# MetaFormer block: groups that stay on their partitions, scores and values in halves

## The reference

```python
x = x + conv(_ln_c(x))             # layer norm over the last axis, j
t = x.reshape(16, 1024, 32)
t = t + ffn(_ln_t(t))              # layer norm over the last axis again

def conv(x, Wq, Wk, Wv, rq, rk, rv, Gq, Gk, Gv1, Gv2):
    q, k, v = (einsum('oc,ncij->noij', W_, x) for W_ in (Wq, Wk, Wv))
    qk  = einsum('ncij,nchj->nihj', q, k) / d
    qrq = einsum('ncij,chi->nihj', q, rq) / d
    krk = einsum('ncij,chi->nihj', k, rk) / d
    weight = softmax(qk + Gq * qrq + Gk * krk, axis=3)      # over j
    return (einsum('nihj,nchj->ncij', weight, Gv1 * v)
            + einsum('nihj,chi->ncij', weight, Gv2 * rv))

def ffn(x, W, V, gamma, beta):
    wx = batch_norm(x @ W.T) * gamma + beta    # statistics over all 16 * 1024 tokens
    yt = sigmoid(wx[:, t] + yt @ V.T)          # one step for each of the 1024 tokens, in order
```

## Time and profile before

| what | value |
|---|---|
| median of three runs | 146.82 us (145.81 to 147.19) |
| the profiled execution's own time | 145.42 us |
| its span in the trace | 143.6 us |
| PE busy | 100.2 us (70%) |
| DVE busy | 99.0 us (69%) |
| ACT busy | 66.0 us (46%) |
| POOL busy | 61.1 us (43%) |

### The profile page before, as it was taken

The page is one execution under the profiler, slowest core; times in us unless marked ns, Lnnn a source line. Parts: engine busy times, 40 slices in busy tenths (PEclk is TensorE's granted clock), DMA queues, the critical chain, the costliest instruction groups (busy, mean ns, idle before and its releaser), DMA issues.

```text
span 143.6 us, 4286 instructions
## 1 busy us (share of the span) xinstructions
PE 100.2 (70%) x1830; PEld 68.2 (47%) x1830; DVE 99.0 (69%) x153; ACT 66.0 (46%) x142; POOL 61.1 (43%) x72
## 2 busy tenths in 40 slices
PE   0697995999299001999975656933998888999200
PEld 0332231388299001999964545301232337999200
DVE  5898838067103899937750199899659879788992
ACT  7958775900063025284030015233533379999300
POOL 8985928840000188990000069982430000005940
PEclk9999999999999955599999999996589999999955
DMA  4892987588800000334642000000000000000667
GB/s 147 264 261 20 208 204 161 132 216 187 205 6 5 5 2 2 77 92 112 164 106 54 5 5 5 0 0 5 0 0 0 0 0 0 5 0 0 188 190 208
DMA packets 9823, 11.63 MB, mean 81 GB/s; under 512 B 2828, under 2 KB 6924, under 8 KB 9804
## 3 DMA queue, kind: packets, MB, share of 16 engines
q1 hardware_dynamic: 9228, 10.31, 28.0%
q10 hardware_dynamic: 576, 1.05, 3.2%
HBM read 2.97 MB, written 2.10 MB: 35 GB/s over the span
## 4 chain that ended last, share of the span: by engine, by line
DVE 29%; PE 27%; ACT 12%; issue 10%; POOL 8%; SPq 6%; DMA 5%; POOLq 0%; ACTq 0%; DVEq 0%
PE ps L1022 6%; PE ps L1001 6%; PE ps L1033 5%; ACT warm L653 5%; PE ps L1055 4%; DVE xin L355 4%; DVE att_tile L742 3%; PE ps L1044 3%; POOL y_tile L433 3%; DVE bn L824 3%; DVE y_tile L361 3%; POOL y_tile L187 3%; SPq L290 3%; DMA xin<-in_x_dram 3%; DMA spread<-att_tile 2%
## 5 line engine op out<-in xcount | busy, mean ns | idle before, releaser
L361 POOL TENSOR_TENSOR y_tile<-xin,u_tile 128x256 f32<-128x256 f32 (+1 forms) x7 | 7.1, 1052 | 24.2 <-DVE xin L355 24.2
L1022 PE MATMUL ps<-w_bd,y_tile 128*32 128x128 f32 x256 | 9.1, 313 | 10.0 <-DVE att_tile L742 10.0
L411 POOL TENSOR_TENSOR att_tile<-att_tile,soft 128x1024 f32<-128x1024 f32 x4 | 7.7, 1914 | 19.5 <-DVE soft L748 19.5
L1055 PE MATMUL ps<-rel_tile,w_bd 128*128 128x512 f32 x16 | 11.1, 806 | 5.2 <-DVE rel_tile L820 5.1
L1022 PEld LDWEIGHTS ps<-w_bd,y_tile 128*32 128x32 f32 x256 | 8.5, 169 | 10.5 <-DVE att_tile L742 10.2
L590 ACT ACTIVATE square<-y_tile 128x512 f32<-128x512 f32 x8 | 5.0, 628 | 18.0 <-POOL y_tile L433 15.9
L1044 PE MATMUL ps<-spread,v_tile 128*32 128x64 f32 x512 | 8.9, 223 | 6.1 <-issue 6.1
L893 DVE TENSOR_SCALAR ps<-att_tile,bnv 128x512 f32<-128x512 f32 x15 | 11.0, 807 | 1.6 <-ACT warm L653 1.6
L1044 PEld LDWEIGHTS ps<-spread,v_tile 128*32 128x32 f32 x512 | 8.1, 109 | 6.9 <-issue 6.9
L1095 PE MATMUL ps<-blank 128*128 128x512 bf16 x48 | 11.3, 382 | 0.0
L968 PE MATMUL ps<-xin 128*128 128x512 f32 x18 | 10.8, 749 | 0.0
(11 more groups left out here) (107 smaller groups left out, 236.7 us busy)
## 6 DMA issues: line engine op xcount, KB each, us to landing
out_dram<-y_tile SPq DMA_DIRECT2D x8, 256.0 KB, 2.4
xin<-in_x_dram SPq DMA_DIRECT2D x3, 512.0 KB, 5.0
spread<-att_tile SPq DMA_DIRECT2D x12, 128.0 KB, 2.5
v_tile<-u_tile SPq DMA_DIRECT2D x12, 128.0 KB, 2.3
spread<-rel_tile SPq DMA_DIRECT2D x24, 64.0 KB, 2.2
xin<-in_x_dram SPq DMA_DIRECT2D x2, 256.0 KB, 2.8
spread<-u_tile SPq DMA_DIRECT2D x4, 128.0 KB, 2.3
v_tile<-u_tile ACTq DMA_DIRECT2D x4, 128.0 KB, 3.9
```

The lines of the kernel that those rows point to most:

```text
L361: return eng.tensor_tensor(result[:, :, rows, :], back[:, at:at + P * k].rearrange("p (q i j) -> p q i j", q=Q, i=k), x2[:, :, rows, :], A ...
L411: nc.gpsimd.tensor_tensor(att_m[:, n, :, :], att_m[:, n, :, :], soft[:, 0, n, :].unsqueeze(2).broadcast_to([P, C, C]), ALU.subtract).then_ ...
L1022: ins = nc.tensor.matmul(bank(n)[group(q), P * k:P * (k + 1)], y[:, q, :, j], w_bd[:, 0, :], start=True, stop=True)
L1055: nc.tensor.matmul(bank(WX_BANK[k % 2]), w_bd[:, 1, :], by_row(tokens, k), start=True, stop=True).then_inc(S["wx_product"], 1)
```

## The change

- `spread_y(q)` puts the copy of group g on the same partitions, block [q, g]; `regroup_u` and the u transfers of ACT are gone (16 transfers of 128 KB).
- The scores are made with the four groups' rows as contraction and the set q as output partitions: the padded block of y against `u_tile` itself. They come in two halves of the rows i: half 0 in banks 2 to 5 before the relative scores, half 1 in banks 0 to 3 after them, and its second part after `score_sum` 2. A matmul has 64 columns, and there are 256 instead of 128.
- `relative_scores` reads the padded blocks too, with 128 rows instead of 32; its copies `rel_out` go from DVE to ACT, behind rv's scaling and the exponential's table.
- Four of the eight `project_values` pieces run before the scores, in banks 0, 1, 6, 7, with copies by DVE; the other four after the scores.
- The weights need only 16 transfers of 128 KB, all on SP, on their own partitions. `weigh` is one instruction for a chunk.
- `relative_values` 0 to 3 and weighted sum 0 run before `relative_values` 4 to 7 and weighted sum 1; they read the padded weights with 128 rows, so they wait for the transfers.
- The order by hand is new: `weight_sum` 0 and 1 ahead of `score_add` 2; `weigh` 0 and 1 ahead of `shift_scores` 2; `value_out` ahead of exp 2; `relv_out` 4 to 7 between the residuals; `t_turn` 0 to 3 one after each of the residuals 4 to 7; four blank matmuls after each of the first four `project_wx`.

```diff
                 for g in range(G):
-                    sp.dma_start(spread4[group(q), q, g, :], turned_y[q][group(g), :]).then_inc(S[f"y_in{q}"], 16)
-            def regroup_u(q): ...
-            def spread_att(k): ...
+                    sp.dma_start(spread4[group(g), q, g, :], turned_y[q][group(g), :]).then_inc(S[f"y_in{q}"], 16)
+            def spread_att(n):
+                wait_weights(sp, n)
+                sp.wait_ge(S["score_b_high"], 1)
+                for q in range(Q):
+                    sp.dma_start(spread4[group(q), n, q, :], rel_tile[group(q), IMG * n:IMG * (n + 1)]
+                                 ).then_inc(S[f"att_in{n // 2}"], 16)
...
-            for k in (0, 1, 2, 3, 4, 6):
-                spread_att(k)
+            for n in range(CHUNKS):
+                spread_att(n)
...
             shift_scores(0)
             shift_scores(1)
+            weigh(0)
+            weigh(1)
             shift_scores(2)
-            weigh(0)
             shift_scores(3)
-            weigh(1)
             weigh(2)
...
             nc.scalar.preload_act_table(ACT.Exp)
+            for n in range(PIECES4):
+                rel_out(n)
             score_exp(0)
             score_exp(1)
-            ...
             value_out(7)
-            spread_att(5)
-            spread_att(7)
+            score_exp(2)
+            score_exp(3)
...
+            def score(half, j, q):
+                first = SCORE_B if half else SCORE_A
+                at = G * HALF * (j % 8)
+                return nc.tensor.matmul(ps[group(q), first + j // 8, at:at + G * HALF].rearrange("p (g i) -> p g i", g=G),
+                                        u[:, q, :, j], y_bd[:, q, :, j // RUN, HALF * half:HALF * (half + 1), j % RUN],
+                                        start=True, stop=True)
...
-            for n in range(PIECES4):
-                relative_scores(n)
-            for q in range(Q):
-                pe.wait_ge(S[f"y_in{q}"], 16 * G)
-            pe.wait_ge(S["u_in"], 16 * G * Q)
-            scores().then_inc(S["score_product"], 1)
+            for n, at in enumerate(EARLY_BANKS):
+                if at == R_BANK:
+                    pe.wait_ge(S["r_ready"], 1)
+                elif at == SIDE[0]:
+                    pe.wait_ge(S["u_half"], 2 * Q)
+                project_values(n, at, "early_product")
+            pe.wait_ge(S["first_beta"], 1)
+            for q in range(Q):
+                pe.wait_ge(S[f"y_in{q}"], 16 * G)
+            scores(0, range(C)).then_inc(S["score_a"], 1)
+            pe.wait_ge(S["early_ready"], EARLY)
+            for n in range(PIECES4):
+                relative_scores(n)
+            scores(1, range(HALF)).then_inc(S["score_b_low"], 1)
+            pe.wait_ge(S["score_sum"], 2)
+            scores(1, range(HALF, C)).then_inc(S["score_b_high"], 1)
+            pe.wait_ge(S["rel_ready"], PIECES4)
+            for n in range(EARLY, PIECES4):
+                project_values(n, n, "value_product")
+            pe.wait_ge(S["rv_set"], 1)
+            pe.wait_ge(S["att_in0"], 16 * Q * 2)
+            for n in range(PIECES4 // 2):
+                relative_values(n)
             pe.wait_ge(S["score_sum"], CHUNKS)
-            ...
+            weighted_sums(0)
+            pe.wait_ge(S["att_in1"], 16 * Q * 2)
+            for n in range(PIECES4 // 2, PIECES4):
+                relative_values(n)
+            weighted_sums(1)
...
-            project_wx(0)
-            project_wx(1)
-            project_wx(2)
-            project_wx(3)
+            for n in range(4):
+                project_wx(n)
+                blank_banks([WARM_BANK] * 4)
```

More of the change, by code:

```diff
@@ L144, in group @@
             return slice(C * g, C * (g + 1))
+        SCORE_A, SCORE_B = 2, 0
         SIDE = [6, 7]
         R_BANK = 0
+        EARLY_BANKS = [0, 1, 6, 7]
+        EARLY = len(EARLY_BANKS)
         WSUM_BANK = [0, 4]
@@ L498, in u_half, with rel_out @@
                 nc.scalar.copy(u_tile[:, IMG * q + BANK * k:IMG * q + BANK * (k + 1)], bank(SIDE[k])).then_inc(S["u_half"], 1)
+            def rel_out(n):
+                rows = slice(ROWS * (n % 4), ROWS * (n % 4 + 1))
+                act.wait_ge(S["rel_product"], n + 1)
+                nc.scalar.copy(rel[:, n // 4, :, rows, :], side_bank(n).rearrange("p (i g j) -> p g i j", i=ROWS, g=G)
+                               ).then_inc(S["rel_ready"], 1)
             def score_exp(n):
@@ L553, in _ @@
             nc.scalar.activation(first_beta, ps[:, 3, 0:1], ACT.Identity, bias=affine[:, 1:2], scale=0.5).then_inc(S["first_beta"], 1)
-            for g in range(G):
-                act.dma_start(v_tile[group(3), IMG * g:IMG * (g + 1)], u_tile[group(g), IMG * 3:IMG * 4]).then_inc(S["u_in"], 16)
             act.wait_ge(S["rv_in"], 16 * G)
@@ L725, in _, with early_out @@
             ln_out(4)
-            def rel_out(n):
-                rows = slice(ROWS * (n % 4), ROWS * (n % 4 + 1))
-                dve.wait_ge(S["rel_product"], n + 1)
-                nc.vector.tensor_copy(rel[:, n // 4, :, rows, :], side_bank(n).rearrange("p (i q j) -> p q i j", i=ROWS, q=Q)
-                                      ).then_inc(S["rel_ready"], 1)
-            for n in range(PIECES4):
-                rel_out(n)
+            def early_out(n):
+                dve.wait_ge(S["early_product"], n + 1)
+                nc.vector.tensor_copy(v_tile[:, BANK * n:BANK * (n + 1)], bank(EARLY_BANKS[n])).then_inc(S["early_ready"], 1)
+            for n in range(EARLY):
+                early_out(n)
             dve.wait_ge(S["rv_scaled"], 1)
@@ L738, in score_add @@
             def score_add(n):
[L739 to L741 removed]
+                first = SCORE_A if n < 2 else SCORE_B
+                if n < 2:
+                    dve.wait_ge(S["score_a"], 1)
+                else:
+                    dve.wait_ge(S["score_b_low"], 1)
+                    dve.wait_ge(S["score_b_high"], 1)
+                dve.wait_ge(S["rel_ready"], PIECES4 // 2 * (n // 2 + 1))
+                gs = slice(2 * (n % 2), 2 * (n % 2) + 2)
                 nc.vector.tensor_tensor(att[:, n, :, :, :],
[L743 removed]
+                                        ps[:, first:first + 4, :].rearrange("p b (j g i) -> p g i (b j)", g=G, i=HALF)[:, gs],
                                         rel_x[:, n, :, :, :], ALU.add).then_inc(S["score_sum"], 1)
@@ L826, in _ @@
             residual(0)
+            relv_out(4)
+            relv_out(5)
             residual(1)
+            relv_out(6)
+            relv_out(7)
             residual(2)
@@ L991, in project_u @@
                     ins.then_inc(S["u_product"], 1)
-            def scores():
-                for j in range(C):
-                    at = Q * C * (j % 4)
-                    if j == 12:
-                        pe.wait_ge(S["first_beta"], 1)
-                    if j // 4 in SIDE and j % 4 == 0:
-                        pe.wait_ge(S["rel_ready"], PIECES4 - 1 + SIDE.index(j // 4))
-                    for g in range(G):
-                        ins = nc.tensor.matmul(ps[group(g), j // 4, at:at + Q * C].rearrange("p (q i) -> p q i", q=Q),
-                                               u_by_q[:, g, :, j], y_bd[:, :, g, j // RUN, :, j % RUN],
-                                               start=True, stop=True)
+            def score(half, j, q):
[4 more added lines that the diff above has]
+                                        start=True, stop=True)
@@ L1004, in scores @@
+            def scores(half, js):
+                for j in js:
+                    for q in range(Q):
+                        ins = score(half, j, q)
                 return ins
             def relative_scores(n):
-                if n < 2:
-                    pe.wait_ge(S["u_half"], 2 * (Q - 1) + n + 1)
-                else:
+                if n >= 2:
                     pe.wait_ge(S["rel_ready"], n - 1)
                 for k in range(ROWS):
-                    for g in range(G):
-                        ins = nc.tensor.matmul(side_bank(n)[group(g), P * k:P * (k + 1)].rearrange("p (q j) -> p q j", q=Q),
-                                               r_fac[group(g), ROWS * n + k, :], y[group(g), :, ROWS * n + k, :],
+                    for q in range(Q):
+                        ins = nc.tensor.matmul(side_bank(n)[group(q), P * k:P * (k + 1)].rearrange("p (g jp t) -> p g jp t", g=G, t=RUN),
+                                               r_fac[:, ROWS * n + k, :], y_bd[:, q, :, :, ROWS * n + k, :],
```

151 lines of the change are left out of this document (53 added, 98 removed).

## The result

The changed kernel takes 149.45 us (median of four runs, 149.44 to 150.55) beside 146.31 us of before (now four runs, 145.79 to 147.19): ratio 1.0227, 95% interval 1.0151 to 1.0303. I had forecast 137.5 us. Its profiled execution has a span of 147.7 us against 143.6.

What follows compares the result with a forecast made beforehand. It took the kernel to be serial in blocks, with TensorE's instruction supply a second limit. Gains of 8.0 us up to residual 4 and 1.3 in the last stage gave 146.8 - 9.3 = 137.5 us, range 134.0 to 142.0 (8 in 10).

Steps and rivals of the forecast that it cites:

- the one on rows: Relative scores and values: going from 32 to 128 rows adds nothing, 8.05 against 8.00 us for 256 records.
- My slower rival: TensorE: gaps bring the clock to 0.50 from the relative scores on, some 17 us against 9.3 gained, 155 us; chance 0.08.
- The supply: TensorE, 64-column matmuls: pages of 256 instructions hold 2.1 us of work but start at least 3.46 us apart.
- The last stage: From residual 4 to complete statistics: new order cuts DVE's idling, 21.3 us instead of 22.70, 1.3 us gained.
- The overlap: Softmax and TensorE blocks overlap: weighted sum 0 done at 70.2 instead of 82.1 us, residual 4 8.0 us earlier.
- rv on ACT's path: ACT's relative-score copies queue behind rv's loads, scaling and table: first can start at 39.05, hidden with 1 us to spare.
- a sign of a late rv: ACT's first relative-score copy after 40.5 us would show the forecast wrong.
- my bounds: Transfers of y before the scores: landing at 32.0, at the other end about 35.5, which costs 2 us.
- eight issues at 0.83 us: SP's weight transfers: 0.6 us an issue taken; at 0.83 it would be 2.3 us more, an end of the range.
- clock falls once: TensorE idles 2.1 us after half 1's values, clock halves, everything from relative values 0 to 3 3.5 us later, 141.0; chance 0.06.
- page I: TensorE's 256 instructions for relative values 0 to 3, waiting for the weight transfers: 59.9 to 63.7 us.
- transfers or pages late: Issues at 0.83 us cost 2.3 us, or pages 4.37 us apart cost 4.7: 139.8 to 142.2 us; chance 0.22.

Runs made afterwards that it cites:

- run 14: Changed kernel with the padded tile's sets 16 KB + 16 bytes apart instead of 16 KB, on one chip with the unaltered changed kernel: 140.14 us, ratio to before 0.9703.
- run 4: Changed kernel with each set's relative-score matmul reading only its own group's 32 partitions, most relative scores left out: 139.92 us in one run.
- run 6: Changed kernel with the padded tile's sets 16 KB + 16 bytes apart instead of 16 KB: 140.86 us.
- run 5: Changed kernel with relative scores reading 128 columns in a row per set instead of short runs, sets still 16 KB apart, scores not computed: 141.12 us in one run.
- run 13: The changed kernel itself, unaltered, timed again on one chip beside the one with 16 bytes more between the sets: 150.45 us, ratio to before 1.0395.
- run 10: Kernel with 16 bytes more between the sets, with three of nine filling matmuls before the projections taken out (12 instructions): 140.37 us, ratio to before 0.9625.
- run 8: Kernel with 128 bytes more between the sets, with the scores' stationary operand read as 32 columns in a row, scores not right: 142.98 us in one run.
- run 3: Changed kernel with four columns put together instead of two: runs of 16 bytes, 512 bytes apart, instead of 8 bytes, 256 apart: 145.16 us.
- run 1: Changed kernel with the padded tile's four sets 16 KB + 128 bytes apart instead of 16 KB, on another chip: 140.28 us.

## Why the prediction was wrong

**The step that failed** is the one on rows: "Relative scores and values go from 32 to 128 rows ... so I add nothing". I gave the relative scores 7.8 us (39.1 to 46.9); they took 17 (40.5 to 57.8), and 7.5 in run 14. The number of rows is nearly free indeed (28.5 ns a record with 32 rows in run 4, 30 to 31 with 128 in runs 6 and 5). But I priced the operation by the earlier trace rows, by scores whose streams walk in steps of 8 bytes, and by relative scores whose streams are on different partitions. No row of before had four streams over the same 128 partitions in short runs. I compared shapes and not address patterns, and put neither a bound nor a rival on the difference. What the runs showed in its place: 64 ns a record instead of 31, and 2 us a copy instead of 0.6, when the four streams' places are equal modulo 256 bytes. My slower rival was the clock, which stayed at 1.00 in this stage; that the kernel came out slower doesn't bear that rival out.

The milestones (us from the span's start): as predicted, in the changed kernel, and in run 14, the same program with the collision taken away.

| | predicted | changed | run 14 |
|---|---|---|---|
| scores half 0 start (y landed) | 32.1 | 33.1 | 34.3 |
| first relative copy | 40.1 | 42.7 | 41.8 |
| `score_add` 0 | 43.7 | 51.1 | 45.2 |
| `score_add` 2 | 53.3 | 65.5 | 55.0 |
| relative values 0 start | 59.9 | 72.2 | 62.7 |
| residual 0 | 70.3 | 85.4 | 74.8 |
| residual 4 | 83.4 | 97.0 | 86.2 |
| statistics complete | 104.8 | 118.2 | 108.8 |

Of the 13.6 us by which residual 4 was late, run 14 takes back 10.9, so I put these to the collision (11.6 by run 13, the changed kernel on run 14's chip, where residual 4 came at 97.8). It acts twice. Pieces 0 to 3 come every 2.1 us instead of 0.9 in run 14, which makes `score_add` 0 5.9 us later; then `score_add` 0 and `score_max` 0 are stretched by 4.8 us. Together that is 10.7 us, against 10.5 measured at `score_add` 2. Half 1 of the scores is late as well, behind pieces 4 to 7 on TensorE, but costs nothing more: it was done at 63.5, while DVE came to `score_add` 2 only at 65.5, and the first transfer of the weights went out at 65.35, as the first `weigh` ended.

**What held.** *The supply:* packets of the 64-column scores start 4.0 and 3.46 us apart; the timeline of TensorE after:

```profile
33.08 3.07 PE L983 MATMUL ps<-spread,u_tile 128*32 128x64 f32 x123 [1.29 <-DMA spread<-att_tile]
37.05 3.06 PE L983 MATMUL ps<-spread,u_tile 128*32 128x64 f32 x128 [0.90 <-issue]
40.51 0.30 PE L983 MATMUL ps<-spread,u_tile 128*32 128x64 f32 x3 [0.40 <-issue]
```

The Trainium skill (Runtime: NRT & Kernel Launch, "Instruction fetch mechanics") calls the cost of crossing a block of 256 instructions mostly hidden. For these matmuls it is not: run 10 shows gaps of 0.95 and 1.78 us that moved with the count of instructions. *The last stage:* 21.1 us, as my own terms add up (19.54 + 1.6; I wrote 21.3), where the clock stays at 1.00. *The overlap:* in run 14 weighted sum 0 is done at 74.7, against 82.1 before. *rv on ACT's path:* the table was loaded at 38.6 (37.36 + 1.28) and was no longer in the way when the first piece came at 42.7. That is past the 40.5 that I had named as a sign of a late rv; rv had come in time, but the relative scores began only at 40.5 and their first piece took 2.1 us.

**Sizes that were off.** SP's eight issues for sets 2 and 3, after, and the loads of rv:

```profile
25.28 5.82 SPq L290 DMA_DIRECT2D spread<-att_tile  x8
31.14 1.97 SPq L322 DMA_DIRECT2D att_tile<-in_L_conv_rv_dram  x4
```

5.82 us instead of 2 x 2.42, and y landed 1 us late here and 2.2 us in run 14, within my bounds. The scores' records took 24 ns, not 17, because of their stationary operand (run 8), which made the gaps shorter and not the time. Each end of a group left 3 to 6 records for the next page, behind a gap that a count in whole pages doesn't see: 0.4 us at the scores and 1.4 at the weighted sums of the changed kernel. In the sum itself, eight issues at 0.83 us instead of 0.6 cost 1.8 us more, not 2.3; they took 0.59 each at the median. The clock fell once as the rival "clock falls once" had it: TensorE stood still for 5.1 us, and the clock was 0.57 in the next window. In the changed kernel this followed from the late softmax; in run 14 it fell as well, after 4.3 us, and page I took 5.1 us. I put the 2.7 us between 83.4 and run 14's 86.2 at residual 4 down to these together; how they share it wasn't measured. In run 14 the last stage then took 22.7 us, with a fall of the clock inside it, so its end is 4.0 us behind the forecast. The repaired kernel's 140.1 us lies in the range that I gave, at the end of my rival "transfers or pages late"; the changed kernel's time doesn't.

**What stays open.** Why 8-byte runs on equal places make TensorE hold up others: the runs show who suffers (PSUM-to-SBUF copies on ACT and DVE, an SBUF-only reduction on DVE) and when, not by what circuit. Whether the 256 bytes belong to the memory or to the distance of the runs, since the distances between the sets were varied with runs 256 bytes apart only. What a stream that starts 8 bytes further shares with its neighbour. And whether the new order of the last stage gains anything in the run time.

## What to carry to other kernels

Price a matmul by the addresses of its moving operand, not by its shape alone: column groups that run together must not read the same partitions in short runs from places that are equal modulo 256 bytes, as tried here with runs 256 bytes apart. A few bytes of padding between the blocks (here 16) were worth 10.3 us, about twice what the rearrangement then gains over the kernel before (145.69 to 140.14 us). When an unrelated engine's copy suddenly costs three times its usual time, look at what TensorE reads at that moment. And count TensorE's instructions in pages of 256: below about 3.5 us of work for a page the supply set the pace here, except right behind a longer page. Cheaper matmuls there saved nothing (run 8), and fewer instructions ahead of them only moved the gap (run 10).

## What the runs showed of the hardware

- Four concurrent column groups over the same 128 partitions, 8-byte runs 256 bytes apart: 64 ns a record when their addresses are equal modulo 256 bytes, 38 ns with 8 bytes between them, 30 ns with 16, 36 ns with 128. In contiguous reads at 16 KB distance: 31 ns. With each stream on 32 partitions of its own: 28.5 ns.
- While that goes on, a 512-column copy out of PSUM takes 2.0 us on ACT and 1.9 us on DVE instead of 0.6 and 0.69, a 1024-column add on DVE 4.67 us instead of 1.20, a reduction from SBUF 2.52 us instead of 1.22. The Trainium skill (SBUF — State Buffer, "SBUF: two separate sides") says that within the engine side only the port pair shared by GpSimd and VectorE causes contention and that TensorE, ScalarE and VectorE's own pair wait on nobody. GpSimd was idle here, so that pair can't be the cause, and the measurement decides: here ScalarE and VectorE were held up.
- A stationary operand whose 32 columns are 128 bytes apart costs 24 to 25 ns a record in 64-column matmuls, against 18 ns for 32 columns in a row (run 8); four such operands were always in use together.
- 16-byte steps of the moving operand in the weighted sums: 30 ns a record against 17 ns with 8-byte steps (run 3). Two of the four streams then lie 256 bytes apart instead of 128, so the step isn't separated from the places.
- Pages of 256 TensorE instructions with 2.1 to 3.1 us of work, one after another, started 3.45 to 4.4 us apart. The first of them behind a page of 128-column matmuls can run on into the second without a gap: 251 records in 4.15 us in run 1, the next page 3.6 us after the second began (an estimate from 69.86 us and half of the 4.15).
